# Layer 1 stores z finished and split; the middle stage loads it ready to use, with four buffers per store

## The reference

```python
def _gat_layer(h, mask, b):
    scores = jnp.einsum('...nd,...md->...nm', h, h)
    scores = jnp.where(mask, scores, NEG)
    attn = jax.nn.softmax(scores, axis=-1)
    return jnp.einsum('...nm,...md->...nd', attn, h) + b
h = jnp.einsum('bnc,hdc->bhnd', x, Wh)                       # 4 heads
out_h = _gat_layer(h, mask[None, None], bh[None, :, None, :])
cat = jnp.transpose(out_h, (0, 2, 1, 3)).reshape(B, N, H * D)
z = jax.nn.leaky_relu(cat, negative_slope=0.2)
h2 = jnp.einsum('bnk,dk->bnd', z, Wo)
out2 = _gat_layer(h2, mask[None], bo)
z2 = jax.nn.leaky_relu(out2, negative_slope=0.2)             # then a layer norm over 64 features
```

## Time and profile before

| | us |
|---|---|
| median of three runs | 3285.74 |
| the three runs | 3283.33, 3285.74, 3295.19 |
| profiled execution, its own time | 3288.88 |
| its span in the trace | 3287.0 |

### The profile page before, as it was taken

One profiled execution on the slowest core, in us unless ns is written; L12 is line 12 of the kernel. 1 busy time (PEld: TensorE's weight loads), 2 busy tenths in 40 slices (PEclk: granted clock), 3 DMA queues, 4 the chain that ended last, 5 costly groups with the idle time before them and its releaser, 6 DMA issues. The chain is left out here.

```text
span 3287.0 us, 124182 instructions
## 1 busy us (share of the span) xinstructions
PE 2949.7 (90%) x49399; PEld 2173.3 (66%) x49399; DVE 2692.0 (82%) x5392; ACT 2273.3 (69%) x2542; POOL 2629.1 (80%) x1463
## 2 busy tenths in 40 slices
PE   5856699999999999999999999999996689999990
PEld 3425577777777777777777777777765556666660
DVE  5764588888888888888888888888877779999997
ACT  2146577777777777777777777777765567777776
POOL 1136598999999999899989999999987878888880
PEclk8989999999999999999999999999998989999995
DMA  5207888999999988998999999989977568988872
GB/s 207 70 1 257 232 159 150 156 171 165 156 161 171 162 157 161 167 164 155 161 165 164 158 160 166 167 156 161 171 123 185 179 141 148 159 154 156 145 135 84
DMA packets 1442513, 514.23 MB, mean 156 GB/s; under 512 B 1359054, under 2 KB 1416844, under 8 KB 1439884
## 3 DMA queue, kind: packets, MB, share of 16 engines
q1 hardware_dynamic: 1442060, 507.32, 80.1%
HBM read 105.27 MB, written 66.06 MB: 52 GB/s over the span
## 5 line engine op out<-in xcount | busy, mean ns | idle before, releaser
L551 POOL TENSOR_TENSOR low<-probs 128x1024 f16<-128x1024 f32 x1280 | 2396.6, 1895 | 331.6 <-ACT probs L829 232.2
L829 ACT ACTIVATE probs<-scores,shifted_max 128x2048 f32<-128x2048 f32 x640 | 1282.5, 2004 | 254.2 <-DVE shifted_max L1038 248.0
L696 PE MATMUL ps<-operands 128*128 128x512 f16 x2560 | 974.4, 381 | 12.9 <-DVE neg_max L1033 7.0
L697 PE MATMUL ps<-operands 128*128 128x512 f16 x2560 | 973.9, 380 | 0.0
L1033 DVE CUSTOM_DVE_ANT_0 scores<-ps,mask 128x1024 f32<-128x1024 f32 x640 | 781.7, 1221 | 207.6 <-PE ps L697 200.0
L842 ACT COPY probsT<-ps 128x1024 bf16<-128x1024 bf16 x640 | 647.4, 1012 | 425.2 <-PE ps L705 421.0
L1033 DVE CUSTOM_DVE_ANT_0 scores<-ps,mask,neg_max 128x1024 f32<-128x1024 f32 x640 | 821.8, 1284 | 132.2 <-issue 83.9
L705 PEld LDWEIGHTS ps<-ident,probs 128*128 128x128 bf16 x10240 | 650.7, 98 | 408.2 <-issue 240.9
L705 PE MATMUL ps<-ident,probs 128*128 128x128 bf16 x10240 | 781.7, 219 | 46.0 <-DVE probsT L1045 39.3
L715 PE MATMUL ps<-v_parts,probsT 128*128 128x64 f16 x10240 | 684.7, 193 | 1.3 <-issue 1.3
L716 PE MATMUL ps<-v_parts,probsT 128*128 128x64 f16 x10240 | 685.1, 193 | 0.0
(11 more groups left out here) (144 smaller groups left out, 1829.9 us busy)
## 6 DMA issues: line engine op xcount, KB each, us to landing
operands<-hT_d SPq DMA_DIRECT2D x40, 512.0 KB, 4.5
operands<-hT_d SPq DMA_DIRECT2D x80, 256.0 KB, 4.4
v_parts<-h_d SPq DMA_DIRECT2D x40, 512.0 KB, 4.4
probsT<-low SPq DMA_TRANSPOSE x1280, 3.6
z_d<-outs SPq DMA_DIRECT2D x38, 512.0 KB, 3.2
scores<-in_adj SPq DMA_DIRECT2D x16, 1024.0 KB, 4.8
h_d<-probs SPq DMA_DIRECT2D x32, 512.0 KB, 3.5
hT_d<-probs SPq DMA_DIRECT2D x32, 512.0 KB, 2.8
```

The costliest lines, as they stand in the source:

```text
L551: pool.tensor_tensor(low[:, u, w], probs[:, u, w], high[:, u, w], ALU.subtract).then_inc(sem(f"low{half}"), 1)
L696: pe.matmul(ps[:, b, :], hi_lo[:, p, t * P:(t + 1) * P], hi_lo[:, p, w], start=True, stop=False)
L697: scored = pe.matmul(ps[:, b, :], hi_lo[:, p, t * P:(t + 1) * P], lo_hi[:, p, w], start=False, stop=True)
L829: act.activation(probs[:, 1 - u, :], scores[:, 1 - u, :], ACT.Exp, bias=shifted_max[:, 1 - u:2 - u], scale=-1.0, accum_out=row_sum[:, held ...
```

## The change

In layer 1 a complete group is no longer finished by line 1060. DVE writes the biased result to a small buffer (`group_tmp`, in `scratch`). ACT multiplies it by 0.2 into the group's PSUM bank (lag 5), DVE takes the maximum of both (lag 5), ACT copies the high f16 half into `outs` (lag 6), and DVE subtracts it and writes the low half beside it (lag 7). The semaphore `out_copied`, on which PE's reuse of the bank and the store of z hang, moves from lag 4 to lag 7, and the steps that empty the pipeline from 5 to 8. `z_d` keeps its size and now holds f16 pairs. The middle stage loads them straight to where PE turns them; the leaky step, the head and the low half are gone from DVE, ACT and POOL there. The load of unit k+4 now waits for PE's turning of unit k. Both stored forms have four buffers, by w. The first four loads are issued before the last store of z. POOL adds beta for all batches in one loop.

```diff
-FLUSH = 5
+FLUSH = 8
...
-        def z_in(w):
-            return (outs[:, 0, :], low[:, 0, :].bitcast(F32), low[:, 1, :].bitcast(F32), outs[:, 1, :])[w]
...
+        def z_halves(held, k, part):
+            return outs[:, held, :].bitcast(F16).rearrange("p (t k d) -> p t k d", k=2, d=D)[:, 4 * k:4 * k + 4, part, :]
+        def group_tmp(k):
+            return scratch[:, k % 2 * 4 * D:(k % 2 + 1) * 4 * D]
...
-        def h2_parts(u):
-            return probsT_hi[:, u, 0, :]
+        def h2_parts(w):
+            return probsT_hi[:, w % 2, w // 2 * 2, :]
...
-                sp.dma_start(z_in(w).rearrange("p (h n) -> p h n", h=H),
+                sp.dma_start(z_parts(w).bitcast(F32).rearrange("p (h n) -> p h n", h=H),
...
-                    sp.wait_ge(sem("p2_zlo"), k + 1)
+                    sp.wait_ge(sem("p2_zT"), k + 1)
...
-            load_z(0, 0)
+            sp.wait_ge(sem("exp_done"), LAYER1 * NT)
+            for w in range(4):
+                load_z(0, w)
             store_z(LAYER1 - 1, 1)
             for u in range(2):
                 for half in range(2):
                     sp.wait_ge(sem(f"low_turned{half}{u}"), turns(LAYER1 * NT - 2 + u, u))
-            load_z(0, 1)
-            load_z(0, 2)
             for u in range(2):
                 sp.wait_ge(sem(f"z_stored{u}"), 8 * LAYER1)
-            load_z(0, 3)
             quads(sp, p2_step)
-            for u in range(2):
-                sp.wait_ge(sem(f"h2_stored{u}"), 8 * UNITS - 16)
-                sp.wait_ge(sem(f"h2T_stored{u}"), 8 * UNITS - 16 * (1 + u))
+            for w in range(4):
+                sp.wait_ge(sem(f"h2_stored{w}"), 4 * UNITS - 16)
+                sp.wait_ge(sem(f"h2T_stored{w}"), 4 * UNITS - 16)
...
-            def p2_step(k, w, b):
-                pool.wait_ge(sem("p2_zhi"), k + 1)
-                gate(pool, "pool")
-                pool.tensor_tensor(z_split(w, 1), z_columns(w), z_split(w, 0), ALU.subtract).then_inc(sem("p2_zlo"), 1)
-                if w == 3:
-                    pool.tensor_tensor(by_tile(x1_of(b)), by_tile(x1_of(b)), parameter(3), ALU.add).then_inc(sem("beta_added"), 1)
-
-            quads(pool, p2_step)
+            with pool.Fori(0, B) as b:
+                pool.tensor_tensor(by_tile(x1_of(b)), by_tile(x1_of(b)), parameter(3), ALU.add).then_inc(sem("beta_added"), 1)
...
-                pe.wait_ge(sem("p2_zlo"), k + 1)
+                pe.wait_ge(sem(f"z_in{w}"), (k - w) * 4 + 16)
...
-                if second and group_at(back, 5):
-                    old, held, k, n = group_at(back, 5)
+                if group_at(back, 5, second) and not second:
+                    old, held, k, n = group_at(back, 5, second)
+                    act.wait_ge(sem("out_biased"), n)
+                    act.activation(group_bank(k), group_tmp(k), ACT.Copy, scale=0.2).then_inc(sem("out_fifth"), 1)
+                if group_at(back, 6, second) and not second:
+                    old, held, k, n = group_at(back, 6, second)
+                    act.wait_ge(sem("out_leaky"), n)
+                    if k == 0:
+                        since(act, sem(f"z_stored{held}"), (old - held) * 8)
+                    act.copy(z_halves(held, k, 0), by_tile(group_bank(k))).then_inc(sem("out_high"), 1)
...
-            def head_z(k, w):
-                act.wait_ge(sem("p2_leaky"), k + 1)
-                since(act, sem("p2_zT"), k - 3)
-                act.copy(z_split(w, 0), z_columns(w)).then_inc(sem("p2_zhi"), 1)
...
-                since(act, sem(f"h2_stored{u}"), stores(k, u))
+                since(act, sem(f"h2_stored{w}"), (k - w) * 4)
+                act.copy(h2_part(w, 0), ps[:, 4 + u, 0:G * D].rearrange("p (s d) -> p s d", s=G)).then_inc(sem("p2_hi"), 1)
...
-                    if k == 0:
+                    if k == 0 and second:
                         gate(dve, "dve")
                         since(dve, sem(f"z_stored{held}"), (old - held) * 8)
                     gate(dve, "dve")
                     for tt in range(4 * k, 4 * k + 4):
-                        added = dve.scalar_tensor_tensor(outs[:, held, tt * D:(tt + 1) * D], out_slot(tt), row_inv[:, held, tt:tt + 1],
+                        added = dve.scalar_tensor_tensor(outs[:, held, tt * D:(tt + 1) * D] if second else group_tmp(k)[:, tt % 4 * D:(tt % 4 + 1) * D], out_slot(tt), row_inv[:, held, tt:tt + 1],
                                                          rows[:, 1, :] if second else bias[:, old, :] if isinstance(old, int) else bias[:, bass.ds(old, 1), :].rearrange("p o d -> p (o d)"),
                                                          ALU.mult, ALU.add)
-                    added.then_inc(sem("n_biased" if second else "out_copied"), 1)
+                    added.then_inc(sem("n_biased" if second else "out_biased"), 1)
...
+            def split_z(back, second):
+                if group_at(back, 5, second):
+                    old, held, k, n = group_at(back, 5, second)
+                    dve.wait_ge(sem("out_fifth"), n)
+                    dve.tensor_tensor(group_bank(k), group_bank(k), group_tmp(k), ALU.max).then_inc(sem("out_leaky"), 1)
+                if group_at(back, 7, second):
+                    old, held, k, n = group_at(back, 7, second)
+                    dve.wait_ge(sem("out_high"), n)
+                    dve.tensor_tensor(z_halves(held, k, 1), by_tile(group_bank(k)), z_halves(held, k, 0), ALU.subtract).then_inc(sem("out_copied"), 1)
...
-            def leaky_z(k, w):
-                dve.wait_ge(sem(f"z_in{w}"), (k - w) * 4 + 16)
-                dve.scalar_tensor_tensor(z_in(w), z_in(w), 0.2, z_in(w), ALU.mult, ALU.max).then_inc(sem("p2_leaky"), 1)
...
-                if within(k + 4):
-                    leaky_z(k + 4, w)
```

More of the change, by code:

```diff
@@ L469, in _ @@
             store_h2T(B - 1, 3)
[L470 to L472 removed]
+            for w in range(4):
+                sp.wait_ge(sem(f"h2_stored{w}"), 4 * UNITS)
+                sp.wait_ge(sem(f"h2T_stored{w}"), 4 * UNITS)
             unrolled(sp, tile_step, LAYER1, B)
```

87 lines of the change are left out of this document (41 added, 46 removed).

## The result

| us | before | after |
|---|---|---|
| median of the runs | 3286.6 (3283.33 to 3295.19) | 3252.11 (3251.1 to 3258.06) |
| ratio, 95% interval | | 0.9899 (0.9877 to 0.9921) |
| span of the profiled execution | 3287.0 | 3249.8 |

The changed kernel is 34.5 us faster in this comparison, against 21.8 forecast. A second comparison of the same two kernels, made with the experiments, gave 3263.27 against 3286.39, ratio 0.9926 (0.9912 to 0.9940), 23.1 us. The table splits three profiled executions at the same events of DVE. "First masking" is the first instruction of L1033 (now L1028) in an instance.

A forecast was written before the change was run, and what follows sets the result against it. PE was taken to bound layer 1 and POOL the middle stage's body; 2.0 - 8.0 - 8.4 - 7.4 = -21.8 us against the runs' median of 3285.74 gave 3263.9, own range 3256 to 3269, 8 in 10 from 3253 to 3277.

The forecast's parts named there:

- The likeliest case: Whole kernel: the forecast of 3263.9 us with its own range, 3256 to 3269, given a chance of 0.74.
- -23.8: Middle stage, last bias to first masking of layer 2: entry, body and exit together 23.8 us shorter.
- Layer 1, +2.0: Layer 1: the added DVE and ACT work hides in gaps behind PE's scores; small disturbances cost 2 us.
- B: Layer 1: the 0.36 us gap is sometimes too small, 11 us beyond the sum, 3274.9; chance 0.11.
- C: Layer 1: DVE comes late for PE, 0.3 us or more a group, 3300 to 3346; chance 0.05, shared with another rival.
- Entry, -8.0: Start of the middle stage: shorter line ahead of PE's first turning, DVE's first split 8.0 us earlier.
- Body, -8.4: Middle stage, first to last split: POOL no longer sets the pace, 3.09 us a unit, 105.3 against 113.7.
- the hole: PE's product where the middle stage's loop ends: a 2.96 us standstill without another engine's work, left in the body.
- four units: Middle stage: some four units run at the lower clock, 1.6 us more each, 6.5 in all.
- made ACT wait: Middle stage stores: two buffers made ACT wait; with four that wait goes too.
- Exit, -7.4: End of the middle stage: waits for stores go, so layer 2's first masking comes 7.4 us earlier; bounds 3.7 to 9.
- PE starts 7.1 us after: Exit: operands go out at about 2624.0 and PE starts layer 2 7.1 us later, at 2631.1.

The follow-up runs named there:

- old finish: Changed kernel with layer 1 finishing as before the change (no leaky step, rounding or split), run twice: 3269.36 us, ratio 0.9937, and 3265.11 us, ratio 0.9941.
- the addition in PSUM: Changed kernel with one more DVE maximum per group of layer 1, first operand in PSUM, ahead of the real maximum: 3261.31 us, ratio 0.9934.
- small beta: Kernel before, with POOL's middle-stage addition of beta applied to one tile of 16 of each batch: 3278.31 us, ratio 0.9965, body 102.83 us.
- two-buffer kernel: Changed kernel with two buffers instead of four for each middle-stage store, and the waits of before at its end: 3314.64 us, ratio 1.0077.

## Why the prediction came out right

The time, 3252.1 in the first comparison and 3263.3 in the second, was forecast as 3263.9. The second is inside my own range of 3256 to 3269. The first is below it, where I had left 0.02, and 0.9 us below my range of 8 in 10, 3253 to 3277. The likeliest case came true by its mechanism, but not each term by its own size. That the middle stage came within 1 to 2 us of its -23.8 is partly luck: in the second profile the body gained 2.8 us more than forecast and the stretch behind it 3.7 less.

**Layer 1, +2.0.** Measured about 0.7 us by the steps other than t = 8, inside their spread. The gaps went as foreseen (0.36 to 0 to 0.05, 0.61 to 0.18). Rivals B and C rested on the gap being all there is; the added 0.42 us that cost nothing shows they had priced slack too low. What would have made C true is an instruction with both inputs in SBUF. The paragraph that asked whether POOL and DVE hold each other up, and found that the new ones have one input in PSUM, carried more than I knew: the same two steps with 1.38 or 1.9 us instructions cost 110 and 122 us.

**Entry, -8.0.** Measured -7.6 and -7.9. Flush, load and chain went as worked out, at the lower clock; in the first profile the whole stands 12 us earlier in the span than I placed it, by as much as layer 1 ended earlier there.

**Body, -8.4.** Measured -6.4, -11.2, -11.4 and -11.8 (old finish) and -9.9 (with the addition in PSUM). The unit of 3.09 was right to 0.03. What moves is the granted clock around the hole: behind it two units of 4.7 us and one of 3.9 in the first profile, one of 3.9 in the second. With those at the start, the units at the low clock cost 6.4 us over the steady ones in the first profile, which is my 6.5 for four units, and 1.6 in the second, which is one. The hole, which I left in at 2.96, costs its unit 4.2 us in both (7.32 and 7.33 against 3.10). So 96.7 + 4.2 + 6.4 is the 107.3 of the first profile and 96.7 + 4.2 + 1.6 the 102.5 of the second; my 105.3 took the four slow units for certain. That POOL was the pace is shown by the kernel with small beta. That the stores "made ACT wait" was true, 12.4 us in ten waits, but POOL's lateness was behind it and not the number of buffers, and the two-buffer kernel shows the size of what that sentence missed.

**Exit, -7.4.** From the split of unit 29 to the first masking: 18.92 before, 13.28 and 14.94 after, so -5.6 and -4.0. The last-split row of the first table shows -7.7 and -3.7; in the first profile the two units ahead of it were slow (8.61 us against 6.54), which is why the row by itself looks better. Here are the exit's rows of the second profile of the changed kernel, DVE, SP and PE:

```profile
2602.48 0.42 DVE L1121 TENSOR_TENSOR probsT<-ps,probsT 128x256 f16<-128x256 f32 x1 [1.59 <-ACT probsT L862]
...
2617.42 1.23 DVE L1028 CUSTOM_DVE_ANT_0 scores<-ps,mask 128x1024 f32<-128x1024 f32 x1 [7.39 <-PE ps L687]
```

```profile
2604.53 0.37 SPq L421 DMA_DIRECT2D h_d<-probsT  x1
2605.20 1.59 SPq L362 DMA_DIRECT2D operands<-hT_d  x3
```

```profile
2615.31 0.61 PE L686 MATMUL ps<-operands 128*128 128x512 f16 x1 [5.74 <-DMA v_parts<-h_d]
```

DVE's removed wait gave what it should: PE's first product to the first masking was 5.64 us and is 1.26 in the first profile and 2.11 in the second. The term that failed is "PE starts 7.1 us after" the operands go out: it took 8.5 and 10.1. SP issues the operands 0.68 us after the store of unit 29 where it took 4.15, which is 3.5 us gained, and 1.4 and 3.0 of that came back in the longer landing. Two stores of 128 KB each now run just ahead of the loads where they had landed before. At the 250 GB/s of the body they take about 1 us, an estimate: most of the 1.4, but not of the 3.0. What the rest is stays open. That these loads were the exit's limit is shown by the two kernels that issue them earlier, with 1.97 and 1.96 us from the last split to the first masking.

**Outside the sum.** In the first comparison 15 us more fell away where I had written "stay as they are". The same kernel profiled again had 375.0, 2110.4 and 558.9 us there, within 2.3 us of before each. So the distance of the first time from the forecast, 12 us, is not a gain that the change is shown to make.

## What to carry to other kernels

Work moved into a stage that another engine bounds costs nothing while it fits, and the room is larger than the gap of one step if the next step has a gap too; but look at where its operands lie before its size, since on DVE two SBUF inputs beside a busy POOL made 0.42 us into 1.4 to 1.9. When a wait is moved on a queue that works in order, ask what stands behind it: here a load's later wait, with two buffers for the stores behind it, made the body 36 to 41 us longer. And profile the changed kernel twice before reading anything into a stretch that the change does not touch.

## What the hardware showed that was not expected

- PE stands still 14 or 15 matmuls into the first product behind the loop of the middle stage, for 2.6 to 3.65 us in thirteen profiles, and for 6.93 where 1.5 MB of loads had been issued 1.9 us ahead of it. One 16 KB packet of the queue `instruction` runs in each of these holes. The Trainium skill, page "Runtime: NRT & Kernel Launch", section "Instruction fetch mechanics", says that engines fetch their instructions by DMA queues of their own; the traces agree, and show that such a fetch can be late behind data transfers (its packet began 4.3 us into the hole, against 0.2 to 1.3).
- The DMAs sustained 250 to 273 GB/s with loads of 512 KB and stores of 128 KB mixed, at a share of 0.85 to 0.91.
- Step 8 of layer 1's instances varied by 8 us in sum from one execution of the changed kernel to another (124.5 and 132.7), which is a third of what the change brings.
